# Six transformer layers rewritten from single heads to half bodies of eight heads on small TensorE tiles

## What is computed

```python
for i in range(DEPTH):                                   # 6
    x = attn_layer(shift_tokens(x), Wqkv[i], ...) + x
    x = ffn_layer(shift_tokens(x), ...) + x

def attn_layer(x, Wqkv, qs, ksc, Wo):
    q, k, v = split(x @ Wqkv)                            # 16 heads of 64 each
    q = l2norm(q) * qs; k = l2norm(k) * ksc
    q = q * cos * scale + rotate_half(q) * sin * scale   # k alike with 1 / scale
    # a window of 32 queries sees its own 32 keys and the 32 before, at most 32 back
    sim = einsum('bhwie,bhwje->bhwij', bq, bk2) * 8.0    # masked, softmax, times values
    return out @ Wo

def ffn_layer(x, g, bln, W1, b1, W2, b2):
    a, gate = split((layernorm(x) * g + bln) @ W1 + b1)   # 341 features each
    return a * gelu(gate) @ W2 + b2
```

## Time and profile before

| | us |
|---|---|
| median of 3 runs | 3387.65 (3383.19 to 3399.04) |
| profiled execution, first to last instruction | 3380.3 |
| median of the runs less this span | 7.4 |
| up to the first projection of the layers | 353 |
| 24 bodies | 2977 |
| last feed-forward and output | 50 |

### The profile page before, as it was taken

The page is one execution under the profiler, slowest core; times in us unless marked ns, Lnnn a source line. Parts: engine busy times, 40 slices in busy tenths (PEclk is TensorE's granted clock), DMA queues, the critical chain, the costliest instruction groups (busy, mean ns, idle before and its releaser), DMA issues.

```text
span 3380.3 us, 58863 instructions
## 1 busy us (share of the span) xinstructions
PE 3232.9 (96%) x19248; PEld 2090.5 (62%) x19248; DVE 2205.7 (65%) x3629; ACT 2309.6 (68%) x3969; POOL 1247.1 (37%) x1137
## 2 busy tenths in 40 slices
PE   5999899999999999999999999999999999999996
PEld 2444566666666666666666666666666666666663
DVE  4444567667667677666766766766766766766763
ACT  2445567777767777766777766777776777776772
POOL 4222333336333345333344333354432354433320
PEclk9688899999999999999999999999998999999997
DMA  3000000111101011110111100111100111100100
GB/s 83 1 2 2 32 35 35 37 38 49 43 35 39 33 40 51 37 39 31 37 43 45 42 35 31 37 48 40 46 33 29 37 48 43 44 29 34 37 32 19
DMA packets 101798, 122.72 MB, mean 36 GB/s; under 512 B 21988, under 2 KB 50786, under 8 KB 101602
## 3 DMA queue, kind: packets, MB, share of 16 engines
q1 hardware_dynamic: 101730, 121.81, 10.3%
HBM read 20.04 MB, written 1.05 MB: 6 GB/s over the span
## 4 chain that ended last, share of the span: by engine, by line
PE 85%; ACT 6%; DVE 4%; issue 3%; POOL 1%; DMA 1%; SPq 0%; DVEq 0%; ACTq 0%; POOLq 0%
PE ring L822 15%; PE ring L844 12%; PE ring L800 5%; PE bank L861 5%; PE ring L820 5%; PE ring L798 4%; PE ring L830 4%; PE ring L810 3%; PE bank L584 3%; PE ring L584 3%; PE bank L768 2%; PE ring L768 2%; PE ring L585 2%; PE ring L586 2%; PE bank L586 2%
## 5 line engine op out<-in xcount | busy, mean ns | idle before, releaser
L514 POOL TENSOR_TENSOR sq_lo<-sq_q,sq_hi 128x512 fp32r<-128x512 f32 x192 | 244.6, 1274 | 1182.3 <-ACT sq_hi L1041 1182.2
L822 PE MATMUL ring<-fin 64*128 64x160 f32 (+1 forms) x3072 | 608.8, 319 | 0.0
L1334 DVE TENSOR_REDUCE neg_max<-ring 128x2 bf16<-128x320 f32 x768 | 357.3, 488 | 275.3 <-PE ring L800 271.0
L844 PEld LDWEIGHTS ring<-probs_t,v_sb 128*128 128x128 f32 x3072 | 469.3, 199 | 72.6 <-issue 33.8
L822 PEld LDWEIGHTS ring<-fin 64*128 64x128 f32 x3072 | 441.5, 188 | 109.9 <-issue 5.5
L844 PE MATMUL ring<-probs_t,v_sb 128*128 128x160 f32 (+1 forms) x3072 | 506.9, 311 | 0.7 <-ACT probs_t L1065 0.7
L1056 ACT ACTIVATE neg_row<-ring 1x512 bf16<-1x512 f32 x384 | 225.1, 586 | 276.2 <-PE ring L810 271.7
L1065 ACT ACTIVATE probs_t<-ring 128x320 f32<-128x320 f32 (+1 forms) x768 | 284.1, 422 | 184.6 <-PE ring L830 184.6
L523 POOL TENSOR_TENSOR rot_k<-tc_k,ts_k 128x512 f32<-128x512 f32 x192 | 258.6, 1347 | 368.3 <-issue 368.2
L1344 DVE TENSOR_TENSOR o_feat<-ring,inv_sums 64x512 f32<-64x512 f32 x384 | 263.5, 686 | 170.8 <-ACT inv_sums L1077 167.9
L523 POOL TENSOR_TENSOR rot_q<-tc_q,ts_q 128x512 f32<-128x512 f32 x192 | 245.3, 1278 | 280.6 <-DMA ts_q<-sr_q 259.2
(11 more groups left out here) (188 smaller groups left out, 6145.2 us busy)
## 6 DMA issues: line engine op xcount, KB each, us to landing
ts_q<-sr_q SPq DMA_DIRECT2D x384, 128.0 KB, 2.0
ts_k<-sr_k SPq DMA_DIRECT2D x384, 128.0 KB, 2.0
w_raw<-in_L_ffn_Wqkv SPq DMA_DIRECT2D x48, 192.0 KB, 2.8
wo_sb<-in_L_ffn_Wo SPq DMA_DIRECT2D x6, 512.0 KB, 4.0
w_raw<-in_L_ffn_W SPq DMA_DIRECT2D x6, 341.0 KB, 3.0
rot_sb<-in_rotary SPq DMA_DIRECT2D x1, 1024.0 KB
out<-x_tok SPq DMA_DIRECT2D x16, 64.0 KB, 1.6
state<-in_blocks SPq DMA_DIRECT2D x1, 768.0 KB
```

The costliest lines, as they stand in the source:

```text
L514: pool.tensor_tensor(sq_lo[:, i, :], sq[i][:], sq_hi[:, i, :].bitcast(F32), ALU.subtract).then_inc(s_sql[i], 1)
L822: pe.matmul(dst[:, at:at + q], k_fin[rows, p % 2, c * P:(c + 1) * P], q_fin[rows, p % 2, c * P:c * P + q], start=False, stop=False)
L844: mm = pe.matmul(dst[:, c * P:c * P + q], v_sb[:, c, p, h * DIM_HEAD:h * DIM_HEAD + P], probs_t[:, h, c * KEYS:c * KEYS + q], start=(c == ...
L1334: dve.tensor_reduce(neg_max[:, h, 2 * b:2 * b + 2], bank[2 + 2 * h + b][:, 0:2 * KEYS].rearrange("p (c k) -> p c k", c=2), AX_X, ALU.max, ...
```

## The change

All of it is in the six layers and in what sets them up. A body is now two **half bodies** of eight heads (four pairs), n = 2 g + a, and each step is done for all eight heads together:

- Projections keep their three matmuls, but q and k of a pair go into one PSUM pair of banks (`ring[0]`), so that one ACT instruction squares 1,024 columns and one DVE instruction multiplies 1,024 columns with a table. The tables are multiplied by the learned scales once in a layer on POOL (`scale_tables`).
- Squares are no longer split: fp32 matmuls with 32 columns of weights, four column places, give the norms of two pairs (`norm2`). The inverse norms then are 8 rows, which a DMA stores in DRAM (`store_norms`) and two DMAs spread over 64 partitions each (`spread_norms`, 1 MB in all).
- The bf16 copies are gone: `max_scores` reads every second bf16 of the fp32 tile. It and `turned_scores` work on blocks of 32 tokens with 64 rows by 32 columns of weights (eight places), 64 columns moving. `attend_local` has 32 rows by 64 columns (eight places). Masks and maxima come in by one matmul of 512 columns for each bank (`pick`).
- Values are projected in plain fp32 with 32 columns of weights, four places (`value_tile`). The sums are made by matmuls of their own (`sum_probs`), inverted on ACT for eight heads at once, stored and spread by DMA (`store_inverses`, `spread_inverses`), and POOL scales (`scale_out`).
- All small results share bank 7 (`N_BANK`), the feed-forward has bank 6 (`F_BANK`).
- The feed-forward of body g - 1 starts in body g (`mine`) and ends in the first half of body g + 1 (`late`). Its products go on from PSUM by one DVE instruction each.
- The shifted input comes by DMA and is split on POOL instead of DVE.

In instructions of PE, a body had 16 x 8 = 128 MATMULs for L822 and as many for L844; it now has 512 and 512, and 256 each for the scores by query and the values.

```diff
@@ PE, squares and values
-            def norm2(n, i, g=None):
-                pe.wait_ge(s_sql[i], n + 1)
-                dst = bank[NORM_BANKS[i]]
-                pe.matmul(dst[:], pair_r[:], sq_hi[:, i, :], start=True, stop=False)
-                pe.matmul(dst[:], pair_r[:], sq_lo[:, i, :], start=False, stop=True).then_inc(s_n2[i], 1)
+            def norm2(n, c):
+                pe.wait_ge(s_sq, 4 * n + 2 * c + 2)
+                ...
+                for t in range(4):
+                    mm = pe.matmul(N_BANK[SLOT * t:SLOT * (t + 1), :], in_head, sq[:, t // 2, t % 2, :],
+                                   start=True, stop=True)
+            def value_tile(g, a, par, t):
+                ...
+                for j in range(4):
+                    for pair in range(GROUP):
+                        at = WINDOW * (4 * t + j)
+                        mm = pe.matmul(N_BANK[SLOT * pair:SLOT * (pair + 1), j * P:(j + 1) * P],
+                                       x_shift[:, par, at:at + WINDOW], wv_sb[:, 4 * a + pair, :], start=True, stop=True)
@@ PE, scores by key and values
-            def turned_scores(n, p, h, between=None):
-                for b in range(2):
-                    pe.matmul(bank[2 + 2 * h + b][:, 0:width], eye16, local_mask_t[:, 0:width], start=True, stop=False)
-                    for dst, c, at, q in spans[2 * b:2 * b + 2]:
-                        pe.matmul(dst[:, at:at + q], k_fin[rows, p % 2, c * P:(c + 1) * P],
-                                  q_fin[rows, p % 2, c * P:c * P + q], start=False, stop=False)
+            def turned_scores(n, a):
+                pe.wait_ge(s_nm, n + 1)
+                for e in range(2):
+                    dst = ring[1 + e]
+                    for h in range(2):
+                        pe.matmul(dst[:, h, :], pick[e][h], key_rows[0:MAX_ROWS + 8, :], start=True, stop=False,
+                                  skip_group_check=True)
+                    for j in range(e, BLOCKS, 2):
+                        at, wide_ = WINDOW * j, queries(j, e)
+                        for pair in range(GROUP):
+                            for h in range(2):
+                                rows = slice(DIM_HEAD * h, DIM_HEAD * (h + 1))
+                                mm = pe.matmul(dst[SLOT * pair:SLOT * (pair + 1), h, at:at + wide_],
+                                               rot[rows, a, pair, 1, at:at + WINDOW], rot[rows, a, pair, 0, at:at + wide_],
+                                               start=False, stop=(j + 2 >= BLOCKS), skip_group_check=True)
+                    mm.then_inc(s_st, 1)
+            def attend_local(n, a):
+                for e in range(2):
+                    for j in range(e, BLOCKS, 2):
+                        for pair in range(GROUP):
+                            for h in range(2):
+                                keys = slice(SLOT * pair, SLOT * (pair + 1))
+                                mm = pe.matmul(bank[2 + pair][DIM_HEAD * h:DIM_HEAD * (h + 1), at:at + wide_],
+                                               v_sb[keys, a, col:col + DIM_HEAD], probs[keys, e, h, at:at + wide_],
+                                               ...)
@@ PE, order of a half body
+                for a in range(2):
+                    project(gn, an, parn, 0)
+                    if a == 0: late.get("g2", nothing)()
+                    value_tile(gn, an, parn, 0)
+                    if a == 1: mine.get("mean", nothing)()
+                    project(gn, an, parn, 1)
+                    if a == 0: late.get("v0", nothing)()
+                    max_scores(n, a)
+                    value_tile(gn, an, parn, 1)
+                    if a == 0: late.get("v1", nothing)()
+                    norm2(n + 1, 0)
+                    project(gn, an, parn, 2)
+                    turn_max(n, end)
+                    (late v2 if a == 0, else mine var)
+                    value_tile(gn, an, parn, 2)
+                    turned_scores(n, a)
+                    (late down if a == 0, else mine g0)
+                    project(gn, an, parn, 3)
+                    if a == 0: mine.get("wo0", nothing)()
+                    value_tile(gn, an, parn, 3)
+                    norm2(n + 1, 1)
+                    sum_probs(n, end)
+                    attend_local(n, a)
+                    (mine wo1 if a == 0, else mine g1)
@@ SP, spreading
+            def store_norms(c, k):
+                sp.wait_ge(s_r, c + 1)
+                ...
+                sp.dma_start(r_rows[k, :, :], r_norm[0:P:SLOT // 2, :]).then_inc(s_rd, 16)
+            def spread_norms(c, k):
+                sp.wait_ge(s_fin, c)
+                sp.wait_ge(s_rd, 16 * (c + 1))
+                for h in range(2):
+                    sp.dma_start(r_all[DIM_HEAD * h:DIM_HEAD * (h + 1), :, :],
+                                 r_rows[k, h:8:2, :].partition_broadcast(DIM_HEAD)).then_inc(s_rb, 16)
@@ POOL, start
             for pair in range(PAIRS):
                 split_pair(0, pair)
+            pool.wait_ge(s_par, 16 * PARAM_LOADS)
+            scale_tables(0, 0)
             for g in range(GROUPS):
                 split_group(g, 0)
```

More of the change, by code:

```diff
@@ L437, in _, with layer @@
+            def layer(l, par, first=False, last=False):
+                for s in range(SEQS):
+                    body(l, s, par, first, last)
+            load_tables(0, 0)
+            load_values(0, 0)
+            load_values(0, 1)
             for pair in range(PAIRS):
@@ L939, in _ @@
+            for key in ("g2", "v0", "v1", "v2", "down"):
+                late[key]()
+            for key in ("wo0", "wo1", "mean", "var", "g0", "g1", "g2", "v0", "v1", "v2", "down"):
+                mine[key]()
             pe.wait_ge(f_x, BODIES + 1)
@@ L1134, in _ @@
[L1134 to L1145 removed]
+                return {"square": square_f, "rstd": rstd_f_, "g0": gate(0), "g1": gate(1), "g2": gate(2), "gelu": gelu}
@@ new lines, in _ @@
+            squares(0, 0)
+            value_out(0, 0, 0)
+            squares(0, 1)
+            value_out(0, 0, 1)
+            rnorm(0)
+            squares(0, 2)
+            value_out(0, 0, 2)
+            squares(0, 3)
+            value_out(0, 0, 3)
+            rnorm(1)
+            body(0, new=False, old=False, first=True)
+            body(1, old=False)
+            with act.Fori(0, BODIES // 2 - 2) as i:
+                body(2 * i + 2)
+                body(2 * i + 3)
+            body(BODIES - 2)
@@ L1384, in product @@
[L1384 to L1390 removed]
+                        n = FFN_TILES[j][1]
```

1187 lines of the change are left out of this document (649 added, 538 removed).

## The result

The changed kernel takes 2954.07 us in the median of 4 runs (2939.66 to 2965.56), the kernel before 3393.18 (3383.19 to 3399.04): a ratio of 0.8711, with a 95% interval of 0.8659 to 0.8763. Forecast were 2840 and a ratio of 0.84, in a range of 2430 to 3400.

A forecast was written before the change was run, and what follows sets the result against it. PE's full queue was taken as the bound: a body 67.3 / 0.78 + 15 = 101 us, 24 bodies 2424 less 50, plus 353 and 9 before, 35 first half body, 50 + 13 last, 7 around: 2840 us, range 2430 to 3400.

The forecast's parts named there:

- PE's work: In a body, PE's matmuls were to take 67.3 us at full clock, where 118.6 were.
- The floor of 25 ns: Rival for a body's 1,536 small matmuls: 0.025 us each at least, time 2840 to 3100; chance 0.10 if following the clock.
- The clock: In the bodies, PE's clock was to average 0.78, between bounds of 0.95 and 0.65, where it was 0.97.
- The waits: New waits of PE in a body: 18 us at full clock, taken as 15.
- the mean: PE's wait before the feed-forward's mean for the sum on DVE, behind the output projection: 6.6 us.
- the term for issue: Long runs of small matmuls: the forecast had no separate issue wait; a rival priced slow issue per instruction, chance 0.11.
- the slower rival: PE issues long runs of 64 small matmuls slower than short ones; at 0.060 us each the time is 4110; chance 0.11.
- over 2.6 us for 64: Trace mark in the runs of L942 and L969: 64 matmuls taking longer than this, with equal gaps, would show slow issue.
- one axis: Rival: array places overlap along rows or columns only, so the 64 batches cost twice, 16 us more; 3320; chance 0.10.
- half clock: Rival: PE's clock at half throughout, a body 135 + 10 us, time 3900; chance 0.04.
- The slow spreading DMAs: Rival: DMAs spreading norms and inverses run at a third of the rate, a body 125 us, no change; chance 0.03.
- One sign of the prediction: Idle time before L1498 was to be ended by POOL or PE's chain, not by r_all's DMA.

The follow-up runs named there:

- e1: Changed kernel with the feed-forward's mid (sum and two copies) moved on DVE ahead of rope 0 and the multiplication by the norms: 2866.4 us, ratio 0.8471.
- e7: Changed kernel with 64 additional transposes on PE ahead of the first projection, shifting its instruction stream by 128 instructions: 2974.26 us, a single run.
- e4: Changed kernel with the DMAs spreading norms and inverse sums writing 32 KB each for 512 KB, so results are wrong: 2801.31 us, ratio 0.8279.
- e9: Kernel of e8 with the spreading DMAs at 32 KB for 512 KB, so results differ: 2515.89 us, ratio 0.7466.
- e3: Changed kernel with PE's loop over four bodies, five times, where it ran over two, ten times: ratio 0.8747.
- e5: Changed kernel with scores by key reordered so eight matmuls in a row use the same place of the array: 3127.89 us, ratio 0.9218.
- e8: Changed kernel with the edits of e1, e6 and e2 together, `down` or `g0` also between the halves of the scores by key: 2766.85 us, ratio 0.8187.
- e6: Changed kernel with POOL's wait for the parameters and first table scaling moved behind the splits of the global attention's third group: 2944.82 us, ratio 0.8687.
- e2: Changed kernel with the runs of scores by key and values times probabilities each cut in two, large matmuls between: 2857.07 us, ratio 0.8455.

## Why the prediction was nearly right

The sum missed by 114 us: 24 bodies at 105.5 for 101 are 108, the start at 374 for 362 is 12. With these in its place, it gives 2954 against a span of 2952.8, so its terms for the first half body, the bodies with less in them and the end held in sum.

**PE's work** was priced at 67.3 at full clock and was 73.6 x 0.85 = 62.6. L867 with 1.0 a group and the value tiles with 1.02 for 1.08 were right. The dear terms were the middles chosen between bounds: scores by query 0.0095 each for 0.018, which is 2.4 for 4.6 a body; by key four runs of 1.47, so 5.9 for 8.0; attend, where the timeline has 190 in 2.39 us (at 1543.39), 6.4 for 8.0. The row for L902, two masks in 0.54, is a little over the 0.22 each taken. The floor of 25 ns, which the Trainium skill gives ("TensorE: Matmul & The Clock Gate", gap of 56 ns), does not hold for matmuls that alternate over eight places: 9.5 and 11.5 ns. The prediction said that the trace agreed so far, but its 0.028 was a mean over 14. In the same trace they start in pairs, 3 to 4 ns apart (313.680 and 313.683), so a closer run was there to be seen.

**The clock** was 0.85 and not 0.78; that alone takes 7 us off the work of a body, the cheaper tiles 5.6.

**The waits** were put at 18, then 15, and are 31.9. Those behind DVE and ACT are 18.3 of these, so the list was right in sum. Within it the mean took 7.8 for 6.6, because its two copies, priced at 0.9, took 1.58 and 0.97 beside POOL's work. The wait of `g0` for DVE (42.6 us in 20 times) was not foreseen, and has the same cause: L1532 took 1956 ns. In e1, where it took 884, that wait is 15.9 us in 4 times. The Trainium skill, "SBUF — State Buffer", in the section on two separate sides, says that VectorE and GpSimd share a pair of ports that one of them holds for a whole instruction; the copies agree, 1.75 us beside POOL and 0.42 without it.

**The step that failed** is the term for issue: nothing in the sum, and a price per instruction in the slower rival. It is neither. It is a stall of about 2 us where one block of instructions ends (e7), up to 6 us where the next block's packet starts late, which the spreading traffic brings about (e4, e9), and 4.4 us behind each jump back (e3): 13.6 us a body. The loop before fetched no instructions, so the rows could show no price for it; what the prediction passed over is that the loop had grown from 1,429 instructions of PE to 6,970. The gaps within runs are equal and short, so the mark "over 2.6 us for 64" would not have found it. The Trainium skill, "Runtime: NRT & Kernel Launch", in the section on instruction fetch, gives blocks of 16 KiB, which agrees with q8, and says that crossing into the next is mostly hidden; here it is not. That the sum came out near is luck, since this miss and those of the clock and of the tiles cancel: 13.6 and 3.3 more, 12.7 less.

Of the rivals, one axis is excluded at its price (4 us for 64 matmuls of L942, 128 instructions, which took 1.47), though e5 does not show by itself that both axes overlap; half clock is excluded by the windows. The slow spreading DMAs did not become the bound (6.7 us for 512 KB, a share of 0.42 in the bodies); their price was paid for the most part in late instructions, 246 us of issue and 251 of time between e8 and e9. One sign of the prediction failed: the idle time of DVE before L1498, 21.0 us in 4 times, was ended by r_all's DMA after all.

What stays open: by which way the traffic delays the blocks. Within two stalls the DMA engines were 0.78 and 1.01 busy (the last windows above). In the 38 stalls over 3 us the packet took 1.24 us in the median and in the 73 between 1 and 2.5 us 0.98, but it started 1.9 us after PE had stopped in the first and 0.75 before in the second. So it is held up before it starts and not under way, which fits a place in line behind other packets; no run tests that. Nor does any tell what size of loop, between 1,429 and 6,970 instructions of PE, is still run without fetching. The start's own part of e6 is open too.

## What to carry to other kernels

Where a rewrite trades few large matmuls for many small ones, count the instructions of a turn of the loop, and look at the page's instruction packets: 43 before, 369 after. If each turn fetches its instructions, price a stall for each block that a run empties faster than the next arrives, and one for each jump back. Put large matmuls between such runs, and keep bulk DMAs from standing in a pile beside them; the two together gave more than either (the gains of e1, e2, e4 and e6 add up to 347 us, and e9, which has all four, gained 438). And ask of each short DVE instruction on the chain what POOL does at that time.

## What the runs showed of the hardware

- Matmuls of 32 columns of weights that alternate over eight places start 9.5 ns (bf16) and 11.5 ns (fp32) apart, with a load of weights for each; on one place the fp32 ones take 52 ns.
- Instructions come in packets of 16.4 KB. A loop of 1,429 instructions of PE ran 21 of its 22 turns without one; a loop of 6,970 took 29 in each turn.
- All 112 stalls on issue over 1 us end 1.2 to 1.8 us after such a packet has landed. They stand multiples of 256 instructions apart and move by 64 matmuls when 64 transposes are put ahead of them. In L942 and L969 they are at most 2.5 us with small spreading DMAs (e4), and up to 6.0 with the full ones.
- Behind the jump back of a loop of 6,970 instructions PE stood for 4.4 us, in 9 of 9 times; with little traffic it was 2.7 (e4) and 3.6 (e9).
- A DVE copy of 64 x 512 takes 0.42 us alone and 1.75 beside POOL.
- The clock in the first stage, with the same code, was 0.89 in one profiled execution and 0.74 in another, and the stage 340 and 386 us long: as much as an edit was worth.
